# A fused attention and FP8-grid feed-forward kernel: down chunks of full height, peaks spread by transposition, fewer warming products and other orders of calls

## What is computed

```python
q = ctx @ Wq.T + bq;  k = ctx @ Wk.T + bk              # ctx: (4, 256, 128)
att = softmax(q @ k.T)                                  # (4, 256, 256)
x = x + layernorm(x) @ att.T
h = layernorm(x).reshape(1024, 256)
qx, sx, sc = quantize(h[:, up_idx])                     # row peaks / 448, rounded to e4m3
g = (qx*sx) @ fp8(w_gate[:, up_idx]).T * sc             # 704 columns, then [:, down_idx]
u = (qx*sx) @ fp8(w_up[:, up_idx]).T * sc               # fp8(W): row peaks, grid, scaled back
t = silu(g) * u
qt, st, sct = quantize(t[:, down_idx])
x = x + (qt*st) @ fp8(w_down[:, down_idx]).T * sct
```

## Time and profile before

| | us |
|---|---|
| runs shown: median (lowest, highest) | 79.89 (79.3, 80.39) |
| the profiled execution, its own time | 79.58 |
| its span, first to last instruction | 77.8 |
| PE / DVE / ACT / POOL busy in it | 69.9 / 61.1 / 56.9 / 49.0 |

### The profile page before, as it was taken

The page is one execution under the profiler, slowest core; times in us unless marked ns, Lnnn a source line. Parts: engine busy times, 40 slices in busy tenths (PEclk is TensorE's granted clock), DMA queues, the critical chain, the costliest instruction groups (busy, mean ns, idle before and its releaser), DMA issues.

```text
span 77.8 us, 1587 instructions
## 1 busy us (share of the span) xinstructions
PE 69.9 (90%) x520; PEld 57.6 (74%) x520; DVE 61.1 (79%) x159; ACT 56.9 (73%) x118; POOL 49.0 (63%) x78
## 2 busy tenths in 40 slices
PE   4999999799959999999999999996989979998940
PEld 4999548589938988999887997984765746676710
DVE  1059899899995999988599999808999999992060
ACT  6106899997899889896899997996288371695400
POOL 5103135369649055987989887899998975853330
PEclk9999999999999999999999999999999999999999
DMA  0999899910000000000000011210240101042204
GB/s 13 272 414 418 258 366 412 409 53 8 0 4 4 0 0 0 0 0 8 0 0 0 34 38 34 67 24 1 85 118 0 67 0 56 11 135 71 70 6 135
DMA packets 4088, 6.98 MB, mean 90 GB/s; under 512 B 656, under 2 KB 2448, under 8 KB 4080
## 3 DMA queue, kind: packets, MB, share of 16 engines
q1 hardware_dynamic: 3888, 6.53, 23.5%
q0 software_dynamic: 192, 0.36, 1.4%
HBM read 5.48 MB, written 1.41 MB: 89 GB/s over the span
## 4 chain that ended last, share of the span: by engine, by line
PE 47%; POOL 22%; ACT 12%; issue 9%; DVE 7%; POOLq 0%; DVEq 0%; ACTq 0%
PE gate_ps L1258 9%; POOL act_g L402 9%; POOL wd_scatter L335 8%; PE tT_ps L1086 7%; PE gate_ps L1162 3%; PE up_ps L1137 3%; PE bank_s L1241 3%; PE tT_ps L1209 3%; PE tT_ps L1073 3%; ACT act_g L591 2%; DVE grid_t L769 2%; PE bank_s L1185 2%; DVE y_sb L892 2%; POOL qxT_bf L395 2%; ACT kT L495 2%
## 5 line engine op out<-in xcount | busy, mean ns | idle before, releaser
L402 POOL TENSOR_TENSOR act_g<-act_g,up_scale 128x704 f32<-128x704 f32 x8 | 13.6, 1695 | 1.1 <-ACT act_g L591 1.0
L1162 PE MATMUL gate_ps<-w_hi,qxT 128*128 128x352 f32 x32 | 11.0, 345 | 0.3 <-ACT act_g L591 0.3
L1209 PE MATMUL tT_ps<-ident,sum_t 128*128 128x128 f32 x48 | 10.4, 283 | 0.3 <-ACT tT L613 0.2
L383 POOL TENSOR_TENSOR sum_w<-sum_w,grid_w 128x256 f32<-128x256 f32 x6 | 4.1, 683 | 10.2 <-DVE sum_w L772 10.2
L1162 PE MATMUL gate_ps<-w_lo,qxT 128*128 128x352 f32 x32 | 10.2, 322 | 0.0
L414 POOL TENSOR_TENSOR x_sb<-y_sb,x 128x256 f32<-128x256 f32 x7 | 6.6, 945 | 5.6 <-DVE y_sb L892 5.6
L857 DVE TENSOR_TENSOR t_sb<-up_ps,act_g 128x704 f32<-128x704 f32 x8 | 7.1, 885 | 3.6 <-POOL act_g L402 2.2
L1212 PE MATMUL tT_ps<-negidentb,grid_t 128*128 128x128 bf16 x48 | 9.6, 219 | 0.0
L613 ACT ACTIVATE tT<-tT_ps 128x768 bf16<-128x768 f32 x7 | 5.7, 808 | 4.9 <-PE tT_ps L1212 4.7
L1086 PE MATMUL tT_ps<-attT,xT 128*128 128x256 f32 x32 | 7.6, 381 | 0.9 <-issue 0.9
L548 ACT ACTIVATE grid_w<-wup_sb,s_w 128x256 bf16<-128x256 f32 x12 | 5.2, 497 | 4.3 <-DVE s_w L808 4.3
(11 more groups left out here) (117 smaller groups left out, 203.6 us busy)
## 6 DMA issues: line engine op xcount, KB each, us to landing
wup_sb<-w_gate_up_dram SPq DMA_DIRECT2D x3, 512.0 KB, 4.8
x_sb<-x_dram SPq DMA_DIRECT2D x4, 256.0 KB, 8.0
xT<-x_t_dram SPq DMA_DIRECT2D x2, 512.0 KB, 9.6
out_dram<-x_sb SPq DMA_DIRECT2D x8, 128.0 KB, 1.7
wdn_sb<-w_down_dram SPq DMA_DIRECT2D x1, 704.0 KB, 6.6
head_sb<-head_dram SPq DMA_DIRECT2D x1, 416.0 KB, 5.4
wdnT<-wd_scatter SPq DMA_DIRECT2D x6, 64.0 KB, 1.9
ctx_sb<-ctx_t_dram SPq DMA_DIRECT2D x1, 256.0 KB, 6.8
```

The lines of the kernel that those rows point to most:

```text
L402: nc.gpsimd.tensor_tensor(act_g[:, i % NT], act_g[:, i % NT], up_scale[:, :], ALU.mult)\
L1162: last = nc.tensor.matmul(ps[:, h, 0:IH], qxT[:, b, c, j * P:(j + 1) * P].bitcast(F32R), w[:, c, a, h * IH:(h + 1) * IH].bitcast(F32R), st ...
L1209: nc.tensor.matmul(to, sum_t[:, i % NT, of], ident[:, :], start=True, stop=False, is_transpose=True)
```

## The change

The down product reads all 128 rows of every chunk. For this the last load back brings its 64 fresh rows only, and GpSimd clears the upper 64 rows of the last chunk (the rows that repeat columns of the fifth are then multiplied by zeros). spread and spread_up use TensorE's transposing form. The warming products are 15, not 24. On SP the first half of x transposed and x of batch 3 move up ahead of the third weight pair and the index; x of batch 1 is still the sixth load. The lists of calls of GpSimd, ScalarE, VectorE and TensorE are partly in another order. The same calls are made on each engine as before, but for the one clearing. An assertion on shapes is shortened.

```diff
-WARM_UP = 24
+WARM_UP = 15
...
-                sp.dma_start(wdnT[:, k], wd_dram[chunk(k), :]).then_inc(wdnT_in, 16)
+                sp.dma_start(wdnT[P - fresh[k]:, k], wd_dram[P * k:P * k + fresh[k], :]).then_inc(wdnT_in, 16)
...
+                nc.gpsimd.memset(wdnT[0:P - fresh[KC - 1], KC - 1], 0.0)
...
                     last = nc.tensor.matmul(spread_ps[:, a], peak_d[:, a:a + 1].to_broadcast([P, P]), ident[:, :],
-                                            start=True, stop=True)
+                                            start=True, stop=True, is_transpose=True)
...
-                                            peak_w[:, k, 1:2].to_broadcast([P, P]), ident[:, :], start=True, stop=True)
+                                            peak_w[:, k, 1:2].to_broadcast([P, P]), ident[:, :], start=True, stop=True,
+                                            is_transpose=True)
...
-                    last = nc.tensor.matmul(y_ps[i], tT[P - fresh[k]:, i % 2, k], wdnT[P - fresh[k]:, k],
+                    last = nc.tensor.matmul(y_ps[i], tT[:, i % 2, k], wdnT[:, k],
...
-                    last = nc.tensor.matmul(y_ps[LAST], tT[P - fresh[k]:, LAST % 2, k], wdnT[P - fresh[k]:, k],
+                    last = nc.tensor.matmul(y_ps[LAST], tT[:, LAST % 2, k], wdnT[:, k],
```

More of the change, by code:

```diff
@@ L420, in _ @@
             subtract_up(0)
+            subtract_up(1)
             diag_up(2)
-            subtract_up(1)
-            diag_up(3)
+            normalise(0)
             subtract_up(2)
-            normalise(0)
             normalise(1)
             add_eps1(0)
+            normalise(2)
             rstd1_of(0)
-            diag_up(4)
[L430 to L435, removed]
+            diag_up(3)
+            subtract_up(3)
+            subtract_up(4)
+            add_eps2(0)
+            rstd2_of(0)
+            normalise(3)
+            diag_up(4)
+            rowscale_of(0)
+            add_eps2(1)
             diag_up(5)
             subtract_up(5)
+            rstd2_of(1)
             add_eps1(1)
-            rowscale_of(0)
-            add_eps2(1)
             rstd1_of(1)
             copy_qxT(0)
-            rstd2_of(1)
             rowscale_of(1)
+            add_eps2(2)
+            rstd2_of(2)
             scale_act(0)
-            add_eps2(2)
+            rowscale_of(2)
+            scale_act(1)
             copy_qxT(1)
-            scale_act(1)
-            rstd2_of(2)
             scale_act(2)
@@ L459, in _ @@
             scale_act(3)
+            copy_qxT(2)
             add_eps2(3)
@@ L638, in _ @@
             evac_up(1)
+            abs_up(4)
             exps(3)
+            evac_attT(1)
+            abs_up(5)
             load_silu()
-            evac_attT(1)
-            abs_up(4)
+            centre_x1(0)
+            evac_attT(2)
             evac_up(2)
-            centre_x1(0)
-            abs_up(5)
-            evac_attT(2)
             evac_up(3)
+            abs_x(0)
+            scale_x(0)
+            centre_x1(1)
             evac_up_scale(0)
-            scale_x(0)
-            abs_x(0)
-            centre_x1(1)
+            evac_up(4)
             evac_up_scale(1)
-            evac_up(4)
             evac_qxT(0)
@@ L1004, in _ @@
             grid_of_t(3)
+            scales_t(4)
             hidden(5)
+            scale_y(0)
             peak_of_t(5)
-            scale_y(0)
+            grid_of_t(4)
             reciprocal_t(5)
-            scales_t(4)
+            sum_of_t(4)
+            scale_y(1)
+            hidden(6)
             scales_t(5)
-            grid_of_t(4)
-            hidden(6)
+            peak_of_t(6)
             grid_of_t(5)
-            scale_y(1)
-            sum_of_t(4)
-            peak_of_t(6)
+            scale_y(2)
             reciprocal_t(6)
-            scale_y(2)
+            sum_of_t(5)
             scales_t(6)
-            sum_of_t(5)
             hidden(7)
@@ L1271, in _ @@
             turn_up(0)
+            turn_up(1)
             turn_att(0)
-            turn_up(1)
             scores(3)
@@ L1295, in _ @@
             gates(2)
+            ups(1)
             turn_down(1, 1)
-            ups(1)
             attend(3)
@@ L1300, in _ @@
             gates(3)
+            ups(3)
             turn_x(2)
@@ L1303, in _ @@
             gates(4)
-            ups(3)
             turn_t(1)
+            turn_t(2)
             gates(5)
             turn_x(3)
-            turn_t(2)
             ups(4)
@@ L1311, in _ @@
             ups(5)
+            down(0)
             gates(7)
-            down(0)
             ups(6)
@@ L1316, in _ @@
             turn_t(3)
-            ups(7)
             down(2)
             turn_t(4)
+            ups(7)
             down(3)
```

139 lines of the change are left out of this document (68 added, 71 removed).

## The result

The median after is 76.21 us (76.17 to 76.5, four runs), before it is 79.92 (79.3 to 80.39, four runs beside them). The ratio is 0.9548, with a 95% interval from 0.9478 to 0.9618: faster by 4.5%. The profiled execution took 76.23 us with a span of 74.4; that of before took 79.58 with 77.8. The forecast was 77.0, its range 75.6 to 79.3. Some executions of a kernel are slower at a lower granted clock, and the ratios leave them out. The kernel before also spreads by over a microsecond from one execution to the next, the one after by 0.3: from lowest to lowest the gain is 3.1 us, not 3.7.

A forecast was written before the change was run, and what follows sets the result against it. Load and VectorE were taken to bound to 33, GpSimd to about 60, then VectorE and TensorE in turn; 1.5 (gates) + 0.7 (scatters) + 0.4 (chunks) + about 0.1 (tail) = 2.7 off 79.58: 77.0, range 75.6 to 79.3.

The forecast's parts named there:

- the 1.5 taken: Up to the gates: the new order starts gates(0) at 31.6 instead of 33.05; bounds nothing to 1.6, VectorE's whole idle time.
- Rival A: The front doesn't move, as VectorE is full and new waits eat the gain: 78.2 or 79.0, given as 78.6; chance 0.22.
- Fifteen warming products: At the start: warming ends at 6.15, projections start at 7.1 instead of 8.14; 0.35 us taken, bounds 0 and 1.04.
- rival B: TensorE's clock falls or rises late between 6.15 and 10.4, costing 1.5: 78.5 us; chance 0.07.
- Peaks by transposition: In spread and spread_up: one pass per block saves 0.9 us of TensorE, partly hidden by its waits for VectorE.
- The scatters' term: GpSimd's row of scatters: rowscale_of(2) and copy_qxT(2) taken out from between them, 0.7 us earlier at scale_act(3).
- the wait in front of turn_t(2): TensorE's new wait in the middle, for evac_tT(1): 0.9 us, costing nothing as GpSimd is then still behind.
- down(0) before gates(7): Weights land at 56.2, TensorE stands 1.5 us from 54.7, scale_act(7) comes at 59.4 instead of 61.18; VectorE loses 0.45.
- Rival C: TensorE stands behind down(0) because its weights still land at 58.4; later work shifts by 1.1: 80.7 us; chance 0.11.
- The tail: Rounding pieces give back up to 1.4, 0.75 lost at scale_y(0) and scale_y(1), 0.5 let go: about 0.1; hidden(7) at 63.8.
- Full chunks: Down products: each of eight about 0.2 shorter without the 64-row stop; six beside VectorE's work, two on the path: 0.4.
- rival D: Transposition keeps both passes and the row count didn't cause the down products' stop: 77.8 us; chance 0.1.

The follow-up runs named there:

- experiment 1: Kernel before with all edits of pieces but its old orders: 78.96 us; with 15 warming products alone: 78.96 us; with the new orders alone: 78.56 us.
- experiment 2: Kernel after with 24 warming products instead of 15: 79.74 us, ratio 0.9896; with 18: 76.48 us, ratio 0.9622.
- experiment 6: Kernel after with the 64-row chunk and old loads back, without the clearing: 79.89 us; with it: 79.83 us. Kernel before with 23 warming products: 79.52 us.
- experiment 5: Kernel after with down(0) behind gates(7) again: 77.55 us; kernel after with only the sixth down product's rows put back to 64: 77.32 us.
- the old chunk's: Kernel after with the 64-row sixth chunk and its old loads back, without the clearing: 79.89 us.

## Why the prediction was right, and which sizes were off

**Direction and the front's mechanism held.** VectorE's idle time in the front was what could be won, and it went from 1.62 to 0.25, 1.37 of the 1.5 taken; the rest of gates(0)'s 2.28 is 0.62 less busy time of VectorE in front of it and 0.29 of the first load. My "above" of 1.6 was therefore no bound. The calls ahead of gates(0) are the same, but their lengths aren't: scales_x(0) took 0.66 before, beside a piece of GpSimd, and 0.16 after, which is 0.5 of the 0.62. I had also given the 1.5 to the orders, with the warming inside it; alone the orders gave 0.76, and the rest came only with the warming and the peaks (experiment 1). Rival A (the front doesn't move) is out.

**Fifteen warming products.** Mis-sized: I gave 0.35, from ScalarE's old pieces. That is about the old order's answer (0.20 to 0.34 at gates(0)); in the new one it is 0.7 to 1.5 (experiment 2). The sum didn't suffer, as the term lay inside the front's 1.5. The products were to end at 6.15: in four of nine profiles with 15 they did (ends from 6.07 to 6.47 with the latency of the last), but in the profiled one of after they kept the low level to the end, at 7.6, and the first projection began at 7.44. I had listed passes of 0.2 us after 6 us as a sign against the forecast. It wasn't one, for VectorE hides the difference. Of rival B the late rise came, but not its price of 1.5: the first projection's pieces of 1.02 are those of before, and behind them the granted clock is 1.00 in the front's windows, with the transposed peaks in them. The Trainium skill, page "TensorE: Matmul & The Clock Gate", Part 4, says that transposes don't count as a busy engine in the same way; in these windows that cost nothing. While TensorE still had work, the granted clock fell in one of the fourteen profiles only, in experiment 6, after TensorE had stood; in five others it fell behind the last product, where it holds nothing up.

**Peaks by transposition.** Eight passes were saved, 2 in spread and 6 in spread_up, as counted: 0.5 at gates(0), 0.1 to 0.3 at the end. "Mostly hidden" held.

**GpSimd.** The new wait was there (1.43), but scale_act(0) began at 35.02, not 34.5, and scale_act(2) at 39.02 (39.2). The scatters' term, 0.7, was mis-sized in both directions: the row got shorter by only 0.2 (40.95 to 49.01 against 42.64 to 50.91), as the gaps of 0.3 stand in the places of the two pieces and the fifth scatter took 1.45 (1.45 or 1.46 in all nine profiles with the unbroken row, without a cause shown), and yet putting the copy back costs 1.15, because there it would wait for ScalarE. One step failed that the sum doesn't show: the wait in front of turn_t(2), 0.99, was to cost nothing because GpSimd is behind. It is on the chain that ended last, and GpSimd isn't. What it costs isn't tested, but the gain of 1.90 at scale_act(3) was 1.2 to 1.4 at hidden(4) and hidden(5).

**down(0) before gates(7).** The step predicted wdnT at 56.2 and TensorE idle for 1.5 us. The wait was 1.3, not 3.3, behind the last scatter, down(0) began at 55.57, and TensorE didn't stand. I had worked with one row of one execution. Rival C is out: under ScalarE's new order the old place is the slower one, by 1.3, through the buffer of tT, a wait that I hadn't looked at.

**The tail.** The rounding piece of 1.44 is back to 0.40 as forecast, and the two ahead of it went from 0.91 and 0.82 to 0.64 and 0.51: 1.6 in all, where I had said up to 1.4. hidden(7) came at 63.28 (63.8), so the 0.5 that I held back wasn't lost.

**Full chunks.** Mis-sized: 0.4 by two stops on the path; measured 0.84 to 1.1. The step "six lie beside VectorE's work" failed. With the other parts in place TensorE is on the chain (PE 32%, DVE 40% of the chain after), and from down(3) on the stops add up. In the old order the step did hold, with 0.32 (experiment 1). The stop itself belongs to the half chunk, as the earlier trace rows suggested; rival D is out.

**The sum.** 77.0 against 76.2. By the milestones of the two profiles the miss is 0.5 more at hidden(7) than in the replay (0.35 of it the full chunks', by experiment 5), the reserve of 0.5 that wasn't needed, and 0.3 less than the 0.4 forecast behind hidden(7). That the sum came so close is in part luck: it added the front, the scatters and the chunks as if each passed to the end, and the front's 1.5 was down to 0.5 at scale_act(0) before other terms made it up.

## What to carry to other kernels

Price an edit in the order in which it will run: nine warming products, the 64-row stops and a copy between scatters were worth 0.35, 0.4 and 0.7 by the old rows, and about 0.7 (at the gates), 0.8 and 1.15 once the other waits around them were gone. A change of milestone isn't a gain before the next shared wait: 0.5 us at the gates vanished at GpSimd's wait for statistics. When one engine's chain is shortened, look which one takes over: here TensorE did, and with it a wait of 0.99 that had been counted as free. And look, before an operation is moved, at who waits for the buffer that it reads, not only at what it waits for.

## What was not expected of the hardware

The clock's rise isn't at a fixed time: with 15 products the thirty passes took 5.01 us in one run (the old chunk's) and 6.54 in another (after), with the same front, while the granted clock column said 1.00 in both; only the lengths of passes tell it. It fell after TensorE had stood 1.74 and 0.99 us, and in another execution with the same gaps it didn't. A 64-row weight load (from partition 64) among 128-row ones stops the loads for 0.21 us, in all eight down products. And the result of a finished product can reach ScalarE 2.1 us late, with no piece in the trace that explains it, in three of the programs run here and not in their neighbours; its cause is open.
